# Time mixing: chunks dealt out one or two to a step, value rows spread as rounded halves, and the bonus added by GpSimd before one centring product

## The chip, the cores and the metric

The kernel runs on one core of a Trainium2 chip. The number compared is device microseconds of one execution. Before the change three executions gave 3112.59, 3116.45 and 3120.53 us, so the median is 3116.45 us. One further execution was profiled: it took 3117.54 us, with a span of 3115.7 us inside it.

## The reference, cut to what matters

The reference is an RWKV-like layer followed by a cross-attention block. Only its first part, time mixing, is touched. Batch is 16, length 128, width 512 in 32 heads of 16.

```python
w = jnp.exp(-jnp.exp(time_decay + jnp.tanh(x5[:, :, 1] @ decay_w1) @ decay_w2))
r = (x5[:, :, 3] @ Wr.T).reshape(b, l, H, S)
k = (x5[:, :, 0] @ Wk.T).reshape(b, l, H, S)
v = (x5[:, :, 2] @ Wv.T).reshape(b, l, H, S)
g = jax.nn.silu(x5[:, :, 4] @ Wg.T)
def step(s, rkvw):
    r_t, k_t, v_t, w_t = rkvw
    a = k_t[:, :, :, None] * v_t[:, :, None, :]
    out = jnp.einsum('bhk,bhkd->bhd', r_t, u * a + s)
    return (a + w_t[:, :, :, None] * s, out)
a4 = att.reshape(b, l, H, S)
m = jnp.mean(a4, axis=-1, keepdims=True)
var = jnp.mean((a4 - m) ** 2, axis=-1, keepdims=True)
att = ((a4 - m) * jax.lax.rsqrt(var + EPS)).reshape(b, l, E) * gn_w + gn_b
x = x + att * g @ Wo.T
```

The part `u * a` of the output is called the bonus in the kernel: r·k·u is summed over a head and multiplied by v.

## The kernel before, in words

`time_mix` works on four batches at a time (a quad, `q` = 0 to 3). A quad has a front (normalisation, the low-rank mixes, the value product `stage`), a **body** of 32 steps `t`, and a joint that finishes quad `q` while it starts quad `q + 1`; after quad 3 there is a closing instead. Channels lie on partitions; the 512 channels make four groups (`g` or `f`, 0 to 3), and steps `8g` to `8g + 7` belong to group `g`. One step handles two of the 16 value rows `d` of a head, for all 512 columns (4 batches x 128 positions).

Each engine has its own program, written out in this order by hand, and they meet by semaphores only. In a step `t` of the body:

- TensorE: `spread(t + 2)` copies two value rows to all partitions of a head: two fp32 products with 32 rows (`tm_spread_v`) into two of the four banks of `tm_vb`. It waits until the scan of step `t` has read these banks (`scanned`). Then come, by a table of conditions on `t`, other pieces: `accumulate(t - 2)` in even steps (sum over the rows of a head, `tm_pick_k`), `bonus(f)` at `8f + 1`, halves (two chunks each) of the projections `receptance`, `key` and `gate` into the one bank `tm_pj1`, `centred(f)` at `8f + 10`, `variance(f)` at `8f + 12`, `unpacks(f)` at `8f + 14`. A chunk is one fp32 product of 128 x 128 by 512 columns, four to a projection. `centred` subtracts the head's mean by a product with `tm_centre`, once for the scan's part (`tm_h5`) and once for the bonus (`tm_bb`), added in PSUM.
- ScalarE: writes the initial state into the banks (`tm_vb<-tm_s`, line 421), which lets VectorE start step `t`. Between these, in order, it takes projections and other results out of PSUM: `bonus(f)` at `8f + 2`, `attended(f)` at `8f + 10`, `square(f)` at `8f + 12`, `deviation(f)` at `8f + 14`, `gate`, `receptance`, `key`.
- VectorE: the product with k (line 567) and two scans (line 572) for each step. After some steps `inverse(f)` (a reciprocal, `8f + 14`) and `gated(f)` (`8f + 15`).
- GpSimd: multiplies the state by r (line 302), and at some steps makes r·k (`receptance_key`) or the bonus product (`bonus`).

The tile `tm_vb` has two pairs of banks, so the values for step `t + 2` can only be spread once step `t` has been scanned. The first and last quads are written out, quads 1 and 2 run in a loop.

Of the kernel before, what the change touches and what calls it, by code (L numbers as in the profile page):

```python
# [25 lines left out]
P = 128  # L26
# [59 lines left out]
def time_mix(nc, io, x2):  # L86
# [3 lines left out]
    with ExitStack() as ctx:  # L90
# [22 lines left out]
        spread_v = sb("spread_v", [P, 4, P])  # L113
        prev = sb("prev", [P, EC, B])
# [56 lines left out]
        vb_full, s0_set, scanned = sem("vb_full"), sem("s0_set"), sem("scanned")  # L171
        rs_ready, rs_used, att_ready = sem("rs_ready"), sem("rs_used"), sem("att_ready")
# [71 lines left out]
        def _(gp):  # L244
# [23 lines left out]

            def bonus(q, f):
                gp.wait_ge(bonus_out, q * 4 + (f + 1))  # L270
                if f < 2 and q > 0:
                    gp.wait_ge(cent_full, q * 4)
                gp.tensor_tensor(quad3(bb[:, f % 2, :]), quad3(ew[:]), vv[:, f, :, 1:L + 1], ALU.mult).then_inc(bonus_used, 1)

            gp.wait_ge(w_ready, 2)
            gp.memset(wd[:], 0.0).then_inc(ready, 1)
            for q in range(NQ):
# [19 lines left out]
                for t in range(STEPS):  # L297
# [5 lines left out]
                    for f in range(EC):  # L303
                        if t == 8 * f - 2:
                            receptance_key(q, f)
                        if t == 8 * f + 2:
                            bonus(q, f)

        @block.scalar
        def _(act):  # L310
# [60 lines left out]
            def body(q, first):  # L371
# [31 lines left out]

                def bonus(f):
# [9 lines left out]
                for f in range(EC):  # L414
                    evacuate(f)
                key(0)
                act.wait_ge(s0_in, q * 16 + 16)
                for t in range(STEPS):
# [5 lines left out]
                    for f in range(EC):  # L424
                        if t == 8 * f + 2:
                            bonus(f)
                        if f > 0 and t == 8 * f - 4:
                            receptance(f)
                        if f > 0 and t == 8 * f - 2:
                            key(f)  # L430
                        if t == (8, 16, 24, 28)[f]:
# [39 lines left out]
        def _(v):  # L471
# [82 lines left out]
            def body(q, first):  # L554
# [5 lines left out]
                for t in range(STEPS):  # L560
# [69 lines left out]
        def _(pe):  # L630
# [68 lines left out]
            def body(q, first):  # L699
# [34 lines left out]
                def spread(t):  # L734
# [1384 lines left out]
```

## Time and profile before

| | us |
|---|---|
| median of 3 executions | 3116.45 (3112.59 to 3120.53) |
| the profiled execution, its own time | 3117.54 |
| its span | 3115.7 |
| body of quad 0, from the first step's product to the last scan | 72.6 to 199.3 |
| body of quad 1 | 258.1 to 387.2 |
| body of quad 2 | 449.2 to 578.3 |
| body of quad 3 | 637.0 to 766.8 |
| end of time mixing, start of the next phase | about 794 |

Over the whole span TensorE is busy 94%, VectorE 58%, ScalarE 37% and GpSimd 15%. These shares are governed by what comes after time mixing and say little of the bodies. In the body of quad 1 (129.1 us) TensorE is busy 113.0 us, VectorE 117.1, GpSimd 82.0 and ScalarE 27.7, at a mean granted TensorE clock of 0.88 of full speed.

### The profile page before, as it was taken

To read this page: it belongs to the slowest core of one execution; us is meant where nothing else is said; L and a number is where in the kernel's file an instruction comes from. 1 tells how busy PE (TensorE), PEld (TensorE's weight loads), DVE (VectorE), ACT (ScalarE), POOL (GpSimd) and SP (SyncE) were. 2 spreads that over 40 slices of the span, in tenths; PEclk is the share of its full clock that TensorE was granted. 3 is DMA by queue.
4 is the path that set the end of the run, shared out by engine and by line. 5 is a ranking of instruction groups with operands and counts; after the bars stand their busy time and mean duration, and the time that the engine had idled before them with its cause. 6 is when DMAs were issued, how large, how long until landed. Compare 5 with 4: busy or idle time off the path is not lost.

```text
span 3115.7 us, 41240 instructions
## 1 busy us (share of the span) xinstructions
PE 2939.4 (94%) x14960; PEld 2212.5 (71%) x14960; DVE 1809.3 (58%) x2660; ACT 1145.5 (37%) x2509; POOL 480.6 (15%) x331
## 2 busy tenths in 40 slices
PE   6889899898696999999999999999999999999899
PEld 3233243332475888888888887878888888888787
DVE  6989979887674544446444456464444554444644
ACT  3222222221343434345343444343434444343432
POOL 1745636455000000001000000010000000000100
PEclk8989899898898999999999999999999999999999
DMA  4000010100224111111111111121111111101011
GB/s 143 7 20 33 11 42 10 32 13 1 97 91 151 65 54 37 54 37 34 52 37 54 37 51 54 47 72 55 37 54 37 54 38 44 47 30 44 27 51 57
DMA packets 54784, 148.76 MB, mean 48 GB/s; under 512 B 6256, under 2 KB 7536, under 8 KB 53584
## 3 DMA queue, kind: packets, MB, share of 16 engines
q1 hardware_dynamic: 51824, 143.80, 13.9%
q0 software_dynamic: 2880, 3.94, 0.6%
q8 instruction: 45, 0.74, 0.1%
q14 instruction: 35, 0.29, 0.0%
HBM read 131.20 MB, written 12.58 MB: 46 GB/s over the span
## 4 chain that ended last, share of the span: by engine, by line
PE 66%; DVE 2%; ACT 1%; issue 0%; DMA 0%; ACTq 0%; DVEq 0%
PE ca_ps L60 19%; PE ca_ps L62 19%; PE ca_ps L61 19%; PE ca_ps L1892 4%; PE ca_ps L1876 4%; PE ca_ps L1884 2%; PE ca_ps L1918 1%; DVE ca_stats L68 0%; DVE ca_xres L1653 0%; DVE ca_ctx_lo L1684 0%; DMA ca_xres<-in_ctxT 0%; DVE ca_wq_lo L1611 0%; ACT ca_sk L1569 0%; DVE ca_h_lo L1678 0%; ACT L1569 0%
## 5 line engine op out<-in xcount | busy, mean ns | idle before, releaser
L1653 DVE TENSOR_TENSOR ca_xres<-ca_xres,ca_ps 128x512 f32<-128x512 f32 x384 | 263.8, 687 | 244.4 <-PE ca_ps L62 239.4
L1440 ACT ACTIVATE ca_pr<-ca_ps,ca_nb 128x129 f32<-128x129 f32 x512 | 181.7, 368 | 510.9 <-DVE ca_nb L1636 510.7
L60 PE MATMUL ca_ps<-ca_h_hi,ca_wq_hi 128*128 128x512 f32 x768 | 313.0, 408 | 4.7 <-DVE ca_h_lo L1678 4.2
L572 DVE TENSOR_TENSOR_SCAN tm_xn<-tm_wd,tm_vb 128x512 f32<-128x512 f32 x256 | 298.5, 1207 | 8.9 <-POOL tm_xf L302 0.4
L62 PE MATMUL ca_ps<-ca_h_hi,ca_wq_lo 128*128 128x512 f32 x768 | 303.0, 394 | 0.0
L61 PE MATMUL ca_ps<-ca_h_lo,ca_wq_hi 128*128 128x512 f32 x768 | 300.9, 392 | 0.0
L60 PE MATMUL ca_ps<-ca_wv_hi,ca_ctx_hi 128*128 128x256 f32 x1024 | 297.8, 291 | 0.0
L62 PE MATMUL ca_ps<-ca_wv_hi,ca_ctx_lo 128*128 128x256 f32 x1024 | 287.4, 281 | 0.0
L61 PE MATMUL ca_ps<-ca_wv_lo,ca_ctx_hi 128*128 128x256 f32 x1024 | 287.2, 280 | 0.0
L60 PE MATMUL ca_ps<-ca_wo_hi,ca_ct_hi 128*128 128x512 f32 x640 | 253.5, 396 | 0.2 <-DVE ca_xres L1653 0.2
L61 PE MATMUL ca_ps<-ca_wo_lo,ca_ct_hi 128*128 128x512 f32 x640 | 252.7, 395 | 0.0
L62 PE MATMUL ca_ps<-ca_wo_hi,ca_ct_lo 128*128 128x512 f32 x640 | 252.5, 394 | 0.0
L1393 POOL TENSOR_TENSOR ca_dv<-ca_bvr 128x256 f32<-128x256 f32 x32 | 23.7, 740 | 1453.7 <-DVE ca_v L1621 1443.7
L60 PE MATMUL ca_ps<-ca_ctx_hi,ca_wk_hi 128*128 128x512 f32 x512 | 203.7, 398 | 22.4 <-DVE ca_wk_lo L1616 18.4
L62 PE MATMUL ca_ps<-ca_ctx_hi,ca_wk_lo 128*128 128x512 f32 x512 | 202.7, 396 | 0.0
L61 PE MATMUL ca_ps<-ca_ctx_lo,ca_wk_hi 128*128 128x512 f32 x512 | 201.4, 393 | 0.0
L746 PE MATMUL tm_vb<-tm_vv,tm_spread_v 32*128 32x512 f32 x512 | 149.9, 689 | 52.2 <-DVE tm_xn L572 52.1
L61 PEld LDWEIGHTS ca_ps<-ca_wv_lo,ca_ctx_hi 128*128 128x128 f32 x1024 | 194.6, 190 | 0.0
L62 PEld LDWEIGHTS ca_ps<-ca_wv_hi,ca_ctx_lo 128*128 128x128 f32 x1024 | 194.1, 190 | 0.0
L60 PEld LDWEIGHTS ca_ps<-ca_wv_hi,ca_ctx_hi 128*128 128x128 f32 x1024 | 192.7, 188 | 0.0
L567 DVE TENSOR_TENSOR tm_vb<-tm_vb,tm_kk 128x1024 f32<-128x1024 f32 x128 | 155.5, 1215 | 33.1 <-ACT tm_vb L421 32.8
L60 PEld LDWEIGHTS ca_ps<-ca_h_hi,ca_wq_hi 128*128 128x128 f32 x768 | 145.1, 189 | 33.6 <-issue 5.4
(233 smaller groups left out, 5832.9 us busy)
## 6 DMA issues: line engine op xcount, KB each, us to landing
ca_sq<-in_wq SPq DMA_DIRECT2D x49, 512.0 KB, 5.4
ca_so<-in_wo SPq DMA_DIRECT2D x48, 512.0 KB, 3.5
ca_sk<-in_wk SPq DMA_DIRECT2D x33, 512.0 KB, 6.6
ca_sv<-in_wv SPq DMA_DIRECT2D x32, 512.0 KB, 3.6
ca_bvr<-in_bvb SPq DMA_DIRECT2D x32, 256.0 KB, 3.9
tm_xq<-in_x SPq DMA_DIRECT2D x16, 256.0 KB, 2.7
tm_xres<-in_x SPq DMA_DIRECT2D x4, 1024.0 KB, 5.7
x_dram<-tm_xres SPq DMA_DIRECT2D x4, 1024.0 KB, 4.6
```

The source lines that it names most:

```text
L60: pe.matmul(out, lhs[0], rhs[0], start=first, stop=False)
L61: pe.matmul(out, lhs[0], rhs[1], start=False, stop=False)
L62: return pe.matmul(out, lhs[1], rhs[0], start=False, stop=last)
L567: v.tensor_tensor(pair4, pair4, kk[:, g:g + 1, :, 0:L].broadcast_to([P, 2, 4, L]), ALU.mult).then_inc(scanned, 1)
L572: v.tensor_tensor_scan(state[t % 2][:, d, :], wd[:, g].rearrange("p b t -> p (b t)"), pair[:, d, :], 0.0, ALU.mult, ALU.add).then_inc(scan ...
L746: ins = pe.matmul(vb[:, 2 * (t % 2) + e, :], spread_v[k:k + 32, u, :], vv[k:k + 32, g, :, 0:L], start=True, stop=True)
L1440: ins = act.activation(pr[hd][:, b, :], ps[:, BANK_SC + b // 2, o:o + KW], ACT.Exp, bias=nbs[hd][:, b:b + 1], scale=SCALE, accum_out=sms[h ...
L1653: v.tensor_tensor(xres[U.h][:, U.quad * 4 + b, :], xres[U.h][:, U.quad * 4 + b, :], ps[:, BANK_O + b % 2, :], ALU.add).then_inc(o_out, 1)
L1876: ins = pe.matmul(ps[:, BANK_SC + b // 2, o:o + KW], qT[hd][:, b * L:(b + 1) * L], kT[hd][:, b, :], start=True, stop=True)
L1884: ins = pe.transpose(ps[:, BANK_TR, b * L:(b + 1) * L], pr[hd][:, b, 0:L], ident[:])
L1892: ins = pe.matmul(ps[:, BANK_PV, b * L:(b + 1) * L], vT[A.quad][:, b, hd * P:(hd + 1) * P], pT[hd][:, b * L:(b + 1) * L], start=True, stop ...
L1918: ins = pe.transpose(ps[:, LN_BANKS[c], b * P:(b + 1) * P], lt[:, b, c * P:(c + 1) * P], ident[:])
```

## The change

Four things move in `time_mix`, all inside the bodies and their ends.

- `spread` for groups 1 to 3 no longer takes fp32 values. ScalarE rounds the value rows to `x_hi` (`value_hi`, at `8f - 6`), GpSimd makes the rest `x_lo` (`value_lo`, at `8f - 5`), and TensorE does four fp32r products of 32 rows instead of two fp32 ones, halves added in PSUM. A rounded copy `spread_r` of the spreading matrix is made once.
- Projections are given out in chunks: at most two in a step, and `receptance`, `key` and `gate` stand one step earlier, or end one step later, than they did.
- GpSimd adds the bonus to the scan's part (`add_bonus`, at `8f + 10`, for group 3 after the last step), and `centred` becomes one product, at `8f + 11`.
- `square`, `variance`, `deviation`, `inverse`, `unpacks` and `gated` stand one step later.

```diff
+            def value_lo(q, c):
+                gp.wait_ge(v_hi_ready, q * 3 + c)
+                gp.tensor_tensor(quad3(x_lo[:, c, :]), vv[:, c, :, 0:L], quad3(x_hi[:, c, :]), ALU.subtract).then_inc(v_split_ready, 1)
+            def add_bonus(q, f):
+                gp.wait_ge(att_ready, q * 4 + (f + 1))
+                gp.wait_ge(bonus_used, q * 8 + (f * 2 + 2 if f < 3 else 6))
+                gp.tensor_tensor(h5[:], h5[:], bb[:, f % 2, :], ALU.add).then_inc(bonus_used, 1)
...
-                    for f in range(EC):
+                    for f in reversed(range(EC)):
                         if t == 8 * f - 2:
                             receptance_key(q, f)
                         if t == 8 * f + 2:
                             bonus(q, f)
+                        if t == 8 * f + 10:
+                            add_bonus(q, f)
+                        if f > 0 and t == 8 * f - 5:
+                            value_lo(q, f)
+                add_bonus(q, 3)
...
+                def value_hi(c):
+                    act.activation(quad3(x_hi[:, c, :]), vv[:, c, :, 0:L], ACT.Copy).then_inc(v_hi_ready, 1)
...
-                        if f > 0 and t == 8 * f - 4:
+                        if f > 0 and t == 8 * f - 5:
                             receptance(f)
+                        if f > 0 and t == 8 * f - 6:
+                            value_hi(f)
...
-                        if t == (8, 16, 24, 28)[f]:
+                        if t == (9, 17, 25, 27)[f]:
                             gate(f)
...
             def centred(q, f):
-                pe.wait_ge(att_ready, q * 4 + (f + 1))
-                pe.wait_ge(bonus_used, q * 4 + (f + 1))
-                pe.matmul(mx[f % 2][:], centre[:], h5[:], start=True, stop=False)
-                pe.matmul(mx[f % 2][:], centre[:], bb[:, f % 2, :], start=False, stop=True).then_inc(cent_full, 1)
+                pe.wait_ge(bonus_used, q * 8 + (2 * f + 3 if f < 3 else 8))
+                pe.matmul(mx[f % 2][:], centre[:], h5[:], start=True, stop=True).then_inc(cent_full, 1)
...
+                        for part in (x_hi, x_lo):
+                            for e in range(2):
+                                k = 32 * (2 * (t % 2) + e)
+                                ins = pe.matmul(vb[:, 2 * (t % 2) + e, :], spread_r[k:k + 32, u, :], part[k:k + 32, g, :],
+                                                start=part is x_hi, stop=part is x_lo)
...
-                        if f > 0 and t in (8 * f - 7, 8 * f - 6):
-                            receptance(f, t - (8 * f - 7))
-                        if f > 0 and t in (8 * f - 5, 8 * f - 4):
-                            key(f, t - (8 * f - 5))
-                        if f < 3 and t in (8 * f + 5, 8 * f + 6):
-                            gate(f, t - (8 * f + 5))
-                        if f == 3 and t in (25, 26):
-                            gate(f, t - 25)
-                        if t == 8 * f + 10:
+                        if f > 0 and t in (8 * f - 8, 8 * f - 7):
+                            receptance(f, ((0, 1), (2, 3))[t - (8 * f - 8)])
+                        if f > 0 and t in (8 * f - 6, 8 * f - 5, 8 * f - 4):
+                            key(f, ((0, 1), (2,), (3,))[t - (8 * f - 6)])
+                        if f < 3 and t in (8 * f + 5, 8 * f + 6, 8 * f + 7):
+                            gate(f, ((0, 1), (2,), (3,))[t - (8 * f + 5)])
+                        if f == 3 and t in (24, 25):
+                            gate(f, ((0, 1), (2, 3))[t - 24])
+                        if t == 8 * f + 11:
                             centred(q, f)
```

TensorE in steps 7 and 8 of a body, before: `spread` (746) for steps 9 and 10, and `accumulate` (666).

```order
L746 MATMUL tm_vb<-tm_vv,tm_spread_v 128x512 [waits tm_scanned]
L746 MATMUL tm_vb<-tm_vv,tm_spread_v 128x512
L746 MATMUL tm_vb<-tm_vv,tm_spread_v 128x512 [waits tm_scanned]
L746 MATMUL tm_vb<-tm_vv,tm_spread_v 128x512
L666 MATMUL tm_mx<-tm_sx,tm_pick_k 32x512 [waits tm_rs_ready]
L666 MATMUL tm_mx<-tm_sx,tm_pick_k 32x512 x3
```

The same two steps now (776 is `spread` by halves, 690 `accumulate`, 782 a chunk of a projection).

```order
L776 MATMUL tm_vb<-tm_x_hi,tm_spread_r 128x512 [waits tm_scanned]
L776 MATMUL tm_vb<-tm_x_hi,tm_spread_r 128x512
L776 MATMUL tm_vb<-tm_x_lo,tm_spread_r 128x512 x2
L782 MATMUL tm_pj<-tm_xg,tm_wg 128x512
L776 MATMUL tm_vb<-tm_x_hi,tm_spread_r 128x512 [waits tm_scanned]
L776 MATMUL tm_vb<-tm_x_hi,tm_spread_r 128x512
L776 MATMUL tm_vb<-tm_x_lo,tm_spread_r 128x512 x2
L690 MATMUL tm_mx<-tm_sx,tm_pick_k 32x512 [waits tm_rs_ready]
L690 MATMUL tm_mx<-tm_sx,tm_pick_k 32x512 x3
L782 MATMUL tm_pj<-tm_xr,tm_wr 128x512 [waits tm_g_ready]
L782 MATMUL tm_pj<-tm_xr,tm_wr 128x512
```

One chunk of gate 0 came into step 7 and two chunks of receptance 2 into step 8, where there were none.

ScalarE around step 10, before: gate 0 (410), the state of steps 9 and 10 (421), `attended(0)` (335), `bonus(1)` (406), the state of steps 11 and 12.

```order
L410 ACTIVATE tm_gg<-tm_pj 128x512 [waits tm_g_full]
L421 ACTIVATE tm_vb<-tm_s 128x8 [waits tm_vb_full] x2
L335 ACTIVATE tm_h<-tm_mx 128x512 [waits tm_bonus_full,tm_rs_used]
L406 ACTIVATE tm_ew<-tm_pj 128x512 [waits tm_bonus_full]
L421 ACTIVATE tm_vb<-tm_s 128x8 [waits tm_vb_full] x2
```

Now (443 is the state, 351 `attended`, 425 `bonus`, 421 `value_hi`, 411 `receptance`).

```order
L429 ACTIVATE tm_gg<-tm_pj 128x512 [waits tm_g_full]
L443 ACTIVATE tm_vb<-tm_s 128x8 [waits tm_vb_full]
L351 ACTIVATE tm_h<-tm_mx 128x512 [waits tm_bonus_full,tm_rs_used]
L425 ACTIVATE tm_ew<-tm_pj 128x512 [waits tm_bonus_full]
L421 ACTIVATE tm_x_hi<-tm_vv 128x512
L443 ACTIVATE tm_vb<-tm_s 128x8 [waits tm_vb_full]
L411 ACTIVATE tm_rr<-tm_pj 128x512 [waits tm_r_full]
```

A third copy, `value_hi(2)`, stands between the bonus and the state of step 11; gate 0 moved from step 8 to step 9.

VectorE at the end of a body, before: the last scan pairs (572), the product of step 31 (567), `inverse(2)` (536), and the joint's first statistics.

```order
L572 SCALAR_TENSOR_TENSOR tm_xn<-tm_wd,tm_vb 128x512
L536 RECIPROCAL tm_grs<-tm_grs 128x128 [waits tm_gstd_ready]
L567 TENSOR_TENSOR tm_vb<-tm_vb,tm_kk 128x1024 [waits tm_s0_set]
L572 SCALAR_TENSOR_TENSOR tm_xn<-tm_wd,tm_vb 128x512 [waits tm_scanned,tm_rs_ready]
L572 SCALAR_TENSOR_TENSOR tm_xn<-tm_wd,tm_vb 128x512
L482 BN_STATS tm_stats<-tm_xq 128x6 [waits tm_x_in0]
```

And now, with lines 591, 596, 560 and 506 in their places.

```order
L596 SCALAR_TENSOR_TENSOR tm_xn<-tm_wd,tm_vb 128x512
L591 TENSOR_TENSOR tm_vb<-tm_vb,tm_kk 128x1024 [waits tm_s0_set]
L596 SCALAR_TENSOR_TENSOR tm_xn<-tm_wd,tm_vb 128x512 [waits tm_scanned,tm_rs_ready]
L596 SCALAR_TENSOR_TENSOR tm_xn<-tm_wd,tm_vb 128x512
L560 RECIPROCAL tm_grs<-tm_grs 128x128 [waits tm_gstd_ready]
L506 BN_STATS tm_stats<-tm_xq 128x6 [waits tm_x_in0]
```

The reciprocal of group 2 moved behind the last scan. TensorE's `unpacks(2)`, which waits for it, stands as before just ahead of the four `output` products that follow the last scan.

## Rows read from the trace of the kernel before

**Rows 1.** The page: span, and the scan's group (mean ns, idle before).
```profile
span 3115.7 us, 41240 instructions
...
L572 DVE TENSOR_TENSOR_SCAN tm_xn<-tm_wd,tm_vb 128x512 f32<-128x512 f32 x256 | 298.5, 1207 | 8.9 <-POOL tm_xf L302 0.4
```

**Rows 2.** VectorE's waits, 72.6 to 766.8 us: total us, times, longest.
```profile
DVE tm_vb L567 <- ACT tm_vb L421: 32.8, 28, 2.2
...
DVE tm_pj L541 <- PE tm_pj L690: 4.1, 8, 0.7
...
DVE tm_xn L572 <- POOL tm_xf L302: 0.4, 2, 0.2
```

**Rows 3.** The same view of quad 1's body alone.
```profile
DVE tm_vb L567 <- ACT tm_vb L421: 9.2, 8, 1.9
```

**Rows 4.** Timeline of VectorE, products of steps 25, 26, 27, quad 1: start, us.
```profile
358.71 1.21 DVE L567 TENSOR_TENSOR tm_vb<-tm_vb,tm_kk 128x1024 f32<-128x1024 f32 x1
...
362.20 1.21 DVE L567 TENSOR_TENSOR tm_vb<-tm_vb,tm_kk 128x1024 f32<-128x1024 f32 x1
...
367.71 1.23 DVE L567 TENSOR_TENSOR tm_vb<-tm_vb,tm_kk 128x1024 f32<-128x1024 f32 x1 [1.93 <-ACT tm_vb L421]
```

**Rows 5.** Timeline of TensorE and ScalarE there; an fp32 product shows as x2.
```profile
362.34 2.08 PE L746 MATMUL tm_vb<-tm_vv,tm_spread_v 32*128 32x512 f32 x4 [1.19 <-DVE tm_xn L572]
...
364.35 2.08 PE L732 MATMUL tm_pj<-tm_h,tm_head_sum_u 128*128 128x512 f32 x2
...
366.52 0.60 ACT L335 ACTIVATE tm_h<-tm_mx 128x512 f32<-128x512 f32 x1 [6.31 <-PE tm_pj L732]
367.01 0.59 ACT L406 ACTIVATE tm_ew<-tm_pj 128x512 f32<-128x512 f32 x1
...
367.49 0.19 ACT L421 ACTIVATE tm_vb<-tm_s 128x8 f32<-128x8 f32 x1
```

**Rows 6.** Timeline of TensorE, steps 9 and 10 of quad 0, at full clock.
```profile
108.67 1.13 PE L746 MATMUL tm_vb<-tm_vv,tm_spread_v 32*128 32x512 f32 x4 [1.44 <-DVE tm_xn L572]
109.73 1.13 PE L732 MATMUL tm_pj<-tm_h,tm_head_sum_u 128*128 128x512 f32 x2
110.69 1.88 PE L751 MATMUL tm_pj<-tm_xr,tm_wr 128*128 128x512 f32 x4
112.50 1.13 PE L746 MATMUL tm_vb<-tm_vv,tm_spread_v 32*128 32x512 f32 x4
113.56 1.07 PE L666 MATMUL tm_mx<-tm_xf,tm_pick_k 128*32 128x512 f32 x8
```

**Rows 7.** Timeline of TensorE, two fp32r products of the value stage, full clock.
```profile
251.62 0.39 PE L61 MATMUL tm_vb<-tm_x_lo,tm_w_hi 128*128 128x512 f32 x1
251.85 0.39 PE L62 MATMUL tm_vb<-tm_x_hi,tm_w_lo 128*128 128x512 f32 x1
```

**Rows 8.** Windows: PE, PEld, DVE, ACT, POOL busy, then granted clock.
```profile
261.70:265.10 3.40, 1.29 (x5) 0.30 (x4) 3.37 (x4) 0.78 (x2) 2.20 (x2) 1.00 0.00 0
...
292.40:295.80 3.40, 2.03 (x14) 0.46 (x12) 3.37 (x4) 0.18 (x1) 2.26 (x2) 1.00 0.00 0
295.80:299.20 3.40, 3.40 (x7) 1.18 (x4) 2.89 (x3) 0.22 (x1) 2.25 (x2) 0.50 0.00 0
```

**Rows 9.** Groups by line, 60 to 770 us, GpSimd and ScalarE: busy, mean ns.
```profile
L302 POOL TENSOR_TENSOR tm_xf<-tm_xn,tm_rr 128x1024 f32<-128x1024 f32 x64 | 150.4, 2352 | 96.2 <-DVE tm_xn L572 73.3 <-PE tm_mx L666 22.9
...
L273 POOL TENSOR_TENSOR tm_bb<-tm_ew,tm_vv 128x512 f32<-128x512 f32 x16 | 18.9, 1181 | 0.0
...
L329 ACT ACTIVATE tm_x_hi<-tm_xf 128x512 fp32r<-128x512 f32 x12 | 7.6, 631 | 37.1 <-DVE tm_xf L520 37.1
```

**Rows 10.** Timeline of the end of quad 1's body and the joint's start.
```profile
382.74 0.93 DVE L536 RECIPROCAL tm_grs<-tm_grs 128x128 f32<-128x128 f32 x1
...
383.75 2.08 PE L690 MATMUL tm_pj<-tm_grs,tm_unpack 128*128 128x128 f32 x8
...
387.21 5.76 PE L695 MATMUL tm_vb<-tm_wo,tm_vv 128*128 128x512 f32 x8 [1.39 <-DVE tm_xn L572]
```

More of the change, by code:

```diff
@@ L113, in time_mix @@
         spread_v = sb("spread_v", [P, 4, P])
+        spread_r = sb("spread_r", [P, 4, P], FR)
         prev = sb("prev", [P, EC, B])
@@ L415, in body @@
                     evacuate(f)
+                if first:
+                    act.wait_ge(const_in, N_CONST)
+                    act.activation(spread_r[:], spread_v[:], ACT.Copy).then_inc(w_hi_ready, 1)
                 key(0)
@@ L740, in spread, with project, key @@
                     elif t % 8 == 0:
-                        pe.wait_ge(f_free, q * 4 + (g + 1))
+                        pe.wait_ge(v_split_ready, q * 3 + g)
+                        if first and g == 1:
+                            pe.wait_ge(w_hi_ready, 4)
                     if t >= 2:
                         pe.wait_ge(scanned, q * (3 * STEPS) + 3 * (t - 1))
-                    for e in range(2):
-                        k = 32 * (2 * (t % 2) + e)
-                        ins = pe.matmul(vb[:, 2 * (t % 2) + e, :], spread_v[k:k + 32, u, :], vv[k:k + 32, g, :, 0:L], start=True, stop=True)
+                    if g == 0:
+                        for e in range(2):
+                            k = 32 * (2 * (t % 2) + e)
+                            ins = pe.matmul(vb[:, 2 * (t % 2) + e, :], spread_v[k:k + 32, u, :], vv[k:k + 32, 0, :, 0:L], start=True, stop=True)
+                    else:
+                        for part in (x_hi, x_lo):
+                            for e in range(2):
+                                k = 32 * (2 * (t % 2) + e)
+                                ins = pe.matmul(vb[:, 2 * (t % 2) + e, :], spread_r[k:k + 32, u, :], part[k:k + 32, g, :],
+                                                start=part is x_hi, stop=part is x_lo)
                     ins.then_inc(vb_full, 1)
-                def project(w, x, f, half, full):
-                    for c in (2 * half, 2 * half + 1):
+                def project(w, x, f, chunks, full):
+                    for c in chunks:
                         ins = pe.matmul(pj[1][:], w[:, c, f * P:(f + 1) * P], x[:, c, :], start=c == 0, stop=c == EC - 1)
-                    if half == 1:
+                    if EC - 1 in chunks:
                         ins.then_inc(full, 1)
-                def key(f, half):
-                    if half == 0:
+                def key(f, chunks):
+                    if 0 in chunks:
                         if f > 0:
@@ L763, in key, with receptance @@
                                 pe.wait_ge(wkr_in, 32)
-                    project(wk, xk, f, half, k_full)
-                def receptance(f, half):
-                    if half == 0:
+                    project(wk, xk, f, chunks, k_full)
+                def receptance(f, chunks):
+                    if 0 in chunks:
                         if f > 1:
@@ L774, in receptance, with gate @@
                             pe.wait_ge(xf_ready, q * 24 + 24)
-                    project(wr, xr, f, half, r_full)
-                def gate(f, half):
-                    if half == 0:
+                    project(wr, xr, f, chunks, r_full)
+                def gate(f, chunks):
+                    if 0 in chunks:
                         if f < 3:
@@ L784, in gate @@
                             pe.wait_ge(late_in, 32)
-                    project(wg, xg, f, half, g_full)
+                    project(wg, xg, f, chunks, g_full)
                 stage(0)
@@ L802, in body @@
                 spread(1)
-                receptance(0, 0)
-                receptance(0, 1)
+                receptance(0, (0, 1, 2, 3))
                 for t in range(STEPS):
```

19 lines of the change are left out of this document (10 added, 9 removed).

## The prediction

> **What bounds the kernel now.** I read the page first. Its busy shares (TensorE 94%) belong to the attention phase, which the change doesn't touch, so I went to time mixing, the first 794 us, and there to the four bodies. In a body VectorE has the longest chain of its own: one product and two scans of 1.21 us a step [rows 1], and when nothing holds it the products of two steps start 3.49 us apart (362.20 - 358.71) [rows 4]. 32 such steps, two reciprocals and two `gated` between them are what a body must take. What it takes beyond that stands in VectorE's waits. Over all four bodies it waits 32.8 us for ScalarE's write of the initial state, 4.1 us for `unpacks`, and 0.4 us for GpSimd [rows 2]; quad 1 alone has 9.2 us of the first kind [rows 3]. These 37.3 us are the most that a change of the other engines' order can give back inside the bodies.
>
> Then I followed one of the waits back. Step 27 of quad 1 started 5.51 us after step 26 instead of 3.49 [rows 4]. Its links, all from [rows 4, 5]: 0.14 us from the end of scan 25 to the start of `spread(27)`, 2.01 until the bonus product can start, 2.08 for that product, 0.09 to ScalarE, 0.49 for `attended`, 0.48 for the bonus copy, 0.22 for the state and the step to VectorE. Together 5.51 us, the measured distance, so nothing else takes part. The state of step 27 isn't late because it needs the bonus; it stands behind it in ScalarE's order, and the bonus product stands behind `spread` in TensorE's. At full clock [rows 6] the first two TensorE links are 1.06 (109.73 - 108.67) and 1.13 us, and the same chain is 0.14 + 1.06 + 1.13 + 0.09 + 0.49 + 0.48 + 0.22 = 3.61 us: a stall of 0.12. So the long stalls are stalls of the granted clock. It fell to half (1.2 GHz) after stretches with little for TensorE to do: after one with 1.29 of 3.40 us busy at the start of quad 1's body, and after 2.03 of 3.40 around steps 8 and 9; the stretch behind the latter ran at 0.50 of full speed [rows 8]. These holes are in the table of steps: before, the steps 7, 8, 15, 16 and 23, 24 have no chunk, and step 0 none either.
>
> **The spread by halves.** Before: two fp32 products in different row strips, 1.06 us to the next instruction at full clock [rows 6]. An fp32 chunk takes 0.90 us (two in 112.50 - 110.69), an fp32r product of the same 512 columns 0.23 (251.85 - 251.62) [rows 6, 7]. The pair costs 1.06 for one product's 0.90, so what is not streaming is about 0.2. Two fp32r products one behind the other in each strip, the strips side by side, are 0.46 + 0.2 = 0.66 us, my value. No row shows an fp32r product in 32 rows. Bounds: 0.46 if the fixed part vanishes, 1.56 if all four run strictly one after the other at their full 0.39 [rows 7]. I take 0.66 because the fp32 pair in these very strips does run side by side.
>
> The Trainium skill (TensorE: Matmul & The Clock Gate, Part 3) says that a weight load goes beside running products only when it is for another row strip. The high and low half share a strip, so by that rule each low product would first wait out its load, and a spread would be nearer 0.9 us. The trace speaks against a full wait: an fp32 product also has two records in the same strip, and the pair still costs only 0.16 more than one chunk. With 0.9 the two chains at steps 11 and 19 are 0.24 longer in each body, about 2 us in all, and the result would be 3096.
>
> **The chunks.** With `accumulate` at 1.00 and `bonus` at 0.96 to the next start [rows 6], TensorE's load now is: step 0: 1.06 + 1.81 = 2.9; steps 8 to 10: 0.66 + about 1.0 + 1.81 = 3.5, just the floor of 3.49; steps 11 to 14: 2.6 to 3.0; steps 15, 16: 2.6 and 3.5; step 7 only 0.66 + 0.90 = 1.6. So the hole at a body's start is filled, and the ones at steps 15 and 23 nearly so, but step 7 keeps one: about 2.0 us busy in 3.4 around it, or less, as in the stretch before the fall at 295.8 [rows 8]. I expect the clock to fall once in each body there, and to come back after one saturated stretch, as the 3.40 us from 295.80 were; at half speed that costs 1.7 us of TensorE's work. Steps 8 and 9 have no slack to make this good, so it arrives whole in step 11.
>
> **ScalarE's third copy.** `value_hi` takes 0.63 us, about 0.50 in a row of copies [rows 5, 9]. It stands ahead of the states of steps 3, 11 and 19. Full-clock chains now: step 11 and 19: 0.14 + 0.66 + 1.13 + 0.09 + 0.49 + 0.48 + 0.50 + 0.22 = 3.71, stall 0.22 each. Step 3 (fp32 spread, no `attended`): 0.14 + 1.06 + 1.13 + 0.09 + 0.50 + 0.50 + 0.22 = 3.64, stall 0.15. Step 27 (no `value_hi`): 3.21, none. With the fallen clock step 11 adds 1.75: 1.97.
>
> **GpSimd.** It gets eight more passes a quad: four adds at about 1.18 and three `value_lo`, at most 1.3 [rows 9]. They are hidden by its idle time: 8 x 2.35 + 4 x 1.2 = 23.6 us in eight steps of at least 27.9. The tight place is steps 10 and 11: counted from scan 10, the products for steps 10, 11 and 12 end at 2.5, 7.2 and 10.9 us (0.15 + 2.35, then bonus, add, 2.35, then `value_lo`, 2.35), and scans 12, 13 and 14 want them at 4.6, 8.1 and 11.6. Nothing waits, with 0.7 us to spare. Behind the add waits `centred`, until 5.0 us; TensorE idles there and the next spread is not due until 7.1. If the cover went, each place would cost about 1 us, 12 in all.
>
> **The later pieces.** `inverse` and `gated` one step later keep their work, but `unpacks` now has a whole step to finish before `gated` wants it, so the 4.1 us go. At a body's end it is the reverse: `inverse(2)` stood before the last scans and now stands behind them, and TensorE must do `unpacks(2)` after it and before the four outputs. The scans end 0.93 earlier, and 2.08 of `unpacks` at half clock come in front of the 5.76 us of outputs and accumulation [rows 10] that the joint waits for: 1.15 us more each for three joints. The closing has the same, less one chunk-sized centring product of 0.90: 0.25. In the joints that product hides behind VectorE's shift chain and gives nothing. Bounds: nothing, if the clock comes back earlier thanks to the added work, and 2.1 us a joint if it comes back one stretch later. The one copy for `spread_r`, 0.6 us, lies in a wait of ScalarE for TensorE.
>
> **The sum.** Given back: 37.3. New stalls for each body: 0.15 + 1.97 + 0.22 = 2.34, and 0.25 for small ones of the kind that the chains don't resolve; four bodies: 10.4. Ends: 3 x 1.15 + 0.25 = 3.7. Net 37.3 - 10.4 - 3.7 = 23.2 us. The profiled execution took 3117.5, which gives 3094.3; the median lies 1.1 us under it, so I forecast 3094, 0.7% less.
>
> **Rivals.**
> 1. The clock holds past step 7. For: in quad 0 the clock stood full at steps 7 to 10, as the full-clock durations of [rows 6] show, although these steps had holes before too. Against: step 7 is emptier than any step next to it. Then 4 x 1.75 fewer: 3087, and some 3 us less if the joints also start at full clock: 3084.
> 2. The clock falls more often. The work that halves take away (0.4 us in 24 steps of a quad) is also what kept TensorE busy; at steps 15 and 23 `unpacks` now waits 0.9 us for the reciprocal in a step that VectorE's own extra work makes 4.4 us long. If the clock falls there too, the chains of steps 19 and 27 get about 1.7 each: 4 x 3.4 = 14 more, 3108.
> 3. The change doesn't reach its purpose because GpSimd's late products bind at steps 12 to 14: 12 places at about 1 us give 3106. Against: the 0.7 us to spare.
> 4. Slower. The four 32-row fp32r products run one after the other. At 1.56 us a spread, eight steps cost TensorE 8 x 1.56 + 4 x 1.0 + 12 x 0.90 + 0.96 + 0.90 and 1.5 for `variance` and `unpacks` = 30.7, with no hole left for waits, and steps 8 to 10 are 4.4 us each. VectorE's own need is 8 x 3.49 + 2.4 = 30.3. The three groups of a body would lose 2.7 us in steps 8 to 10 and again in 16 to 18 and 24, 25, and about as much in the chains at half clock: some 12 us a body against 9.3 now, and with the ends 3129. It decides at a spread of about 1.4 us; below that the filled holes win.
>
> **Chances.** The forecast's way 0.52 (3088 to 3101 alone), rival 1 0.18, rivals 2 and 3 together 0.21, rival 4 0.09. The range goes from rival 1's 3083 to 3109, just past rival 2. A measurement of this kernel tells about 0.3% (9 us) from no change, so faster ends at 3107: the forecast, rival 1 and half of 2 and 3 make 0.80; same 0.13, slower 0.07.
>
> **What would show it.** A spread with about 0.66 us to the next instruction. VectorE's wait for the state down from 32.8 to about 10 us, most of it at step 11, and after a fall of the granted clock around step 8; none at steps 13, 21, 27 and 29. No wait of `gated` for `unpacks` in the bodies. About 1.2 us more from the last scan to ScalarE's `attended(3)`. I am wrong if spreads take over 1 us, if half-clock stretches come at steps 16 and 24, or if VectorE waits for GpSimd by more than 2 us.

## The result and the profile after

| | before | after |
|---|---|---|
| median, us | 3115.75 (4 executions) | 3088.84 (3087.40 to 3094.17, 4 executions) |
| ratio to before | | 0.9916, 95% interval 0.9901 to 0.9932 |
| the profiled execution | 3117.54 | 3094.17, span 3091.6 |
| bodies of quads 0 to 3, us | 126.7, 129.1, 129.1, 129.8 | 122.3, 119.2, 117.0, 121.1 |
| from each body to the next (the last: to the next phase) | 58.8, 62.0, 58.7, 27.5 | 60.6, 64.8, 60.6, 28.6 |
| start of the first body | 72.6 | 75.5 |
| start of the next phase | 794.3 | 769.8 |

By medians the kernel is 0.84% faster, 26.9 us; 3094 with a range of 3083 to 3109 was forecast. The four bodies became 35.1 us shorter, what lies between and behind them 7.6 us longer, and the first body began 2.9 us later. That last difference isn't the change's: the same kernel profiled once more (below) began it at 73.1.

VectorE's waits in time mixing after the change, the view of [rows 2]: total us, times, longest.

```profile
DVE tm_vb L591 <- ACT tm_vb L443: 8.4, 8, 3.3
DVE tm_xn L522 <- PE tm_mx L690: 6.4, 3, 2.6
...
DVE tm_pj L565 <- PE tm_pj L712: 2.2, 1, 2.2
...
DVE tm_xn L596 <- POOL tm_xf L313: 0.4, 2, 0.2
```

The wait for the initial state fell from 32.8 to 8.4 us, and the one for `unpacks` inside the bodies is gone (the single 2.2 stands in the closing). New is 6.4 us in the three joints (line 522), where `output` and `accumulate` come late; before it was 2.6. GpSimd is waited for no more than before.

A stretch in which the granted clock is 0.50 (1.2 GHz) is called a fall from here on, and a step of TensorE with little in it a hole. The fall at the start of a body is gone, as was worked out: before, the clock fell 7 to 8 us into each of the four bodies (at 80.8, 265.1, 456.2 and 644.0 us); now it stays full there in all four, in quad 1 from 258.4 to 292.0 us.

Most of the 8.4 us, 7.2, is left at step 11; the rest is at step 19. TensorE in steps 7 and 8 of quad 0 and at the start of step 9 (start, length, what, idle before):

```profile
104.02 0.50 PE L776 MATMUL tm_vb<-tm_x_hi,tm_spread_r 32*128 32x512 f32 x2 [0.68 <-DVE tm_xn L596]
104.36 0.40 PE L776 MATMUL tm_vb<-tm_x_lo,tm_spread_r 32*128 32x512 f32 x2
104.68 1.12 PE L782 MATMUL tm_pj<-tm_xg,tm_wg 128*128 128x512 f32 x2
107.58 0.70 PE L776 MATMUL tm_vb<-tm_x_hi,tm_spread_r 32*128 32x512 f32 x2 [1.77 <-DVE tm_xn L596]
108.07 0.63 PE L776 MATMUL tm_vb<-tm_x_lo,tm_spread_r 32*128 32x512 f32 x2
108.64 1.94 PE L690 MATMUL tm_mx<-tm_sx,tm_pick_k 128*32 128x512 f32 x8
110.50 3.78 PE L782 MATMUL tm_pj<-tm_xr,tm_wr 128*128 128x512 f32 x4
114.21 0.64 PE L776 MATMUL tm_vb<-tm_x_hi,tm_spread_r 32*128 32x512 f32 x2
```

The first three rows are step 7. The spread takes 104.68 - 104.02 = 0.66 us to the next instruction, then one chunk, then 1.77 us of nothing. From 107.58 to the end of these chunks the products take twice their time: `accumulate` 1.86 us to the next start instead of 1.00, two chunks 3.71 instead of 1.81. ScalarE's copies and VectorE's product of step 11 follow late:

```profile
116.24 0.60 ACT L351 ACTIVATE tm_h<-tm_mx 128x512 f32<-128x512 f32 x1 [7.31 <-PE tm_pj L754]
116.73 0.59 ACT L425 ACTIVATE tm_ew<-tm_pj 128x512 f32<-128x512 f32 x1
117.21 0.63 ACT L421 ACTIVATE tm_x_hi<-tm_vv 128x512 fp32r<-128x512 f32 x1
117.73 0.18 ACT L443 ACTIVATE tm_vb<-tm_s 128x8 f32<-128x8 f32 x1
```
```profile
111.00 1.21 DVE L591 TENSOR_TENSOR tm_vb<-tm_vb,tm_kk 128x1024 f32<-128x1024 f32 x1
...
117.94 1.23 DVE L591 TENSOR_TENSOR tm_vb<-tm_vb,tm_kk 128x1024 f32<-128x1024 f32 x1 [3.30 <-ACT tm_vb L443]
```

It is the chain of [rows 5] again, with `value_hi` as a third copy in it. The windows over these steps (as [rows 8]):

```profile
100.90:104.30 3.40, 2.72 (x16) 0.74 (x14) 3.30 (x4) 0.18 (x1) 3.34 (x3) 1.00 0.02 5
104.30:107.70 3.40, 1.63 (x8) 0.43 (x8) 3.30 (x4) 2.06 (x3) 2.20 (x2) 1.00 0.00 0
107.70:111.10 3.40, 3.40 (x13) 0.99 (x14) 3.30 (x4) 0.18 (x1) 2.33 (x1) 0.50 0.00 0
111.10:114.50 3.40, 3.40 (x6) 0.96 (x6) 3.30 (x3) 0.00 (x0) 2.35 (x1) 0.50 0.00 0
114.50:117.90 3.40, 3.40 (x12) 1.32 (x12) 0.14 (x1) 1.66 (x5) 2.85 (x2) 1.00 0.00 0
```

TensorE is busy 1.63 of 3.40 us around step 7, and the two stretches behind run at 0.50 (1.2 GHz). VectorE waits at step 11 of quads 0 to 3 for 3.30, 1.88, 0.23 and 1.77 us; in quad 2, the one of 0.23, the clock stayed full through these steps, and around the same step 7 TensorE was busy 2.25 and 2.14 of 3.40:

```profile
469.50:472.90 3.40, 2.25 (x8) 0.59 (x6) 3.37 (x4) 1.44 (x2) 3.40 (x3) 1.00 0.00 0
472.90:476.30 3.40, 2.14 (x13) 0.75 (x14) 3.37 (x4) 0.81 (x3) 2.26 (x2) 1.00 0.00 0
```

The end of quad 1's body, TensorE and then VectorE (before: [rows 10]):

```profile
378.49 2.08 PE L712 MATMUL tm_pj<-tm_grs,tm_unpack 128*128 128x128 f32 x8 [3.39 <-DVE tm_grs L560]
380.36 5.50 PE L717 MATMUL tm_vb<-tm_wo,tm_vv 128*128 128x512 f32 x8
385.79 1.07 PE L690 MATMUL tm_mx<-tm_sx,tm_pick_k 128*32 128x512 f32 x8
```
```profile
377.50 0.93 DVE L560 RECIPROCAL tm_grs<-tm_grs 128x128 f32<-128x128 f32 x1
...
387.13 0.18 DVE L522 COPY tm_xn<-tm_prev 128x16 f32 x1 [2.55 <-PE tm_mx L690]
```

The reciprocal is now behind the last scan, TensorE stands idle for it, and `unpacks` and the outputs run at half clock until the joint's VectorE has waited 2.55 us.

### The profile page after: what moved, and what is told of

Read it like the earlier page. It is cut to its first block, busy times and chain, and to the rows that moved or that the text cites. A ratio compares the mean times of both kernels' runs of the same rounds, so it can differ in the third digit from the quotient of the medians.

```text
span 3091.6 us, 41223 instructions
## 1 busy us (share of the span) xinstructions
PE 2888.0 (93%) x14928; PEld 2196.8 (71%) x14928; DVE 1805.6 (58%) x2660; ACT 1150.9 (37%) x2522; POOL 514.6 (17%) x359
## 4 chain that ended last, share of the span: by engine, by line
PE 66%; DVE 2%; ACT 1%; issue 0%; DMA 0%; ACTq 0%; DVEq 0%
PE ca_ps L60 19%; PE ca_ps L62 19%; PE ca_ps L61 19%; PE ca_ps L1922 4%; PE ca_ps L1906 4%; PE ca_ps L1914 2%; PE ca_ps L1948 1%; DVE ca_stats L68 0%; DVE ca_xres L1683 0%; DVE ca_ctx_lo L1714 0%; DMA ca_xres<-in_ctxT 0%; DVE ca_wq_lo L1641 0%; ACT ca_sk L1599 0%; DVE ca_h_lo L1708 0%; ACT L1599 0%
## 5 line engine op out<-in xcount | busy, mean ns | idle before, releaser
L62 PEld LDWEIGHTS ca_ps<-ca_h_hi,ca_wq_lo 128*128 128x128 f32 x768 | 144.8, 189 | 33.3
L61 PEld LDWEIGHTS ca_ps<-ca_h_lo,ca_wq_hi 128*128 128x128 f32 x768 | 145.3, 189 | 28.1
```

What stands on the lines that cost most here:

```text
L61: pe.matmul(out, lhs[0], rhs[1], start=False, stop=False)
L62: return pe.matmul(out, lhs[1], rhs[0], start=False, stop=last)
```

## Experiments: the parts of the change

Each version is an edit of the changed kernel, or of the one before where said. The kernel before was timed beside each of three sets: its median was 3115.24 beside the changed kernel again, step 7 with two chunks, the early inverse and all three together; 3115.85 beside the four versions that take the change apart; 3114.68 beside the other four. The four versions that take the change apart ran on another chip than the other eight, beside the kernel before there. "State wait" is VectorE's wait for the initial state, the first row of the view above; the "period" of a step is the time from the product of the step before to its own. Medians whose intervals overlap are called apart only where the trace shows where they part.

**The changed kernel again**, no edit.

> The changed kernel once more, beside the variants. Its median was 3088.8 us, four runs from 3087.4 to 3094.2, and in its profile the falls of the granted clock decide the wait at step 11 (3.30, 1.88, 0.23 and 1.77 us in quads 0 to 3). If the falls are a matter of where the chip's clock stands against the program, this run gives 3086 to 3094 with other numbers at the steps 11, sum 5 to 10 us; if they are fixed by the program, the same four numbers come back within 0.1 us.

3087.95 us, 0.9916 (0.9902 to 0.9929), span 3081.7. State wait 6.2 us; the periods of step 11 are 5.31, 5.46, 3.81 and 5.44, and the first clock fall behind step 7 was 3.4 us long and not 6.8. The numbers of step 11 did not all come back, so the program alone does not fix where the falls lie and how long they last. Two profiles of one kernel differ by 2.2 us in the state wait and 2.4 in the opening, and one version below, with the same steps 0 to 29, had 12.7 us: a state wait from one profile says little, medians more.

**Only the halves**: the kernel before, with `value_hi`, `value_lo`, `spread_r` and the four fp32r products.

```diff
-    for e in range(2): matmul(vb, spread_v, vv[.., g, ..])
+    for part in (x_hi, x_lo):
+        for e in range(2): matmul(vb, spread_r, part[.., g, :])
```

> Only the spreads by halves, in the old table. TensorE has 0.4 us less to do in 24 steps of a quad, and the holes at steps 7, 8, 15, 16, 23 and 24 become emptier. If holes and the clock rule: the falls stay or come oftener, waits of 1.5 to 2 us at steps 11, 19, 27 remain, the 4.1 us for the unpacking remain, time 0 to 8 us under the kernel before. Rival (TensorE's load rules): 12 us or more under it.

3097.63 us, 0.9946 (0.9928 to 0.9964). State wait 22.5 us in 21 places, none longer than 1.6; the falls stay where they were, at the chains of steps 11, 19 and 27:

```profile
DVE tm_vb L583 <- ACT tm_vb L435: 22.5, 21, 1.6
```

In the old table halves alone give 18 us, where 0 to 8 were expected and the rival said 12 or more. The falls behaved as expected; what they cost did not. At half clock a spread by halves took 1.06 us to the next start (107.58 to 108.64 above), where the whole one took 2.01 [rows 5], so each chain behind a fall is shorter. The wait of `gated` for `unpacks`, expected to remain, is gone too, with `unpacks` at its old step.

**Whole fp32 spreads**: the changed kernel without the halves.

```diff
-    act value_hi at 8f - 6, POOL value_lo at 8f - 5, four fp32r products
+    two fp32 products for all groups
```

> The changed kernel with fp32 spreads for all groups, no value_hi and value_lo. A spread then costs 1.06 us instead of 0.66 to the next instruction. If the halves pay for themselves (steps 8 to 10 hold 1.06 + 1.0 + 1.8 = 3.9 us of work against 3.49, so the lag grows by 0.4 a step): waits of 1 to 2 us at steps 11, 19 and 27, time 6 to 12 us over the changed kernel. Rival (more streaming keeps the clock up, and the third copy is gone): no falls behind step 7, the waits of step 11 shrink, time within 3 us of the changed kernel or under it.

3084.85 us, 0.9904 (0.9882 to 0.9925). State wait 7.3 us in 5 places, the longest 3.7. The halves gave nothing on top of the new table, where 6 to 12 us had been expected of them. The rival's time held, and its reason in part: behind step 7 the clock still fell in quads 0 (6.8 us) and 3 (3.4 us).

**Two centring products**: `add_bonus` taken out, `centred` as before but at its new step.

```diff
-    matmul(mx, centre, h5 + bb)
+    matmul(mx, centre, h5, start=True, stop=False)
+    matmul(mx, centre, bb, start=False, stop=True)
```

> The changed kernel with the bonus added in PSUM by a second centring product again, no add on GpSimd. The second product costs TensorE 0.9 us in steps 11, 19 and 27, which hold 2.6 to 3.0 us of work, so it fits. Expectation: no wait in the bodies grows by more than 0.2 us, the time is within 2 us of the changed kernel, 1 us more at the closing. Rival (the single product is what made room): waits at steps 12 and 20, 5 us or more slower.

3089.6 us, 0.992 (0.9899 to 0.9941). State wait 9.1. No difference in time that can be told, as expected.

**Only the table**: both edits together, so that of the change the dealing of chunks and the later places are left.

> Only the new places of chunks and later pieces: fp32 spreads, two centring products. If the filled steps and the room before gated are most of the gain: 12 to 20 us under the kernel before. Rival (the halves are most of it): under 8 us.

3087.36 us, 0.9912 (0.9891 to 0.9933). State wait 8.4 us, in 4 places, the longest 3.8. The numbers in the table alone give all of the gain: 28.5 us, where the whole change gives 26.9 and 12 to 20 had been expected. Halves and table take from the same waits: of the 32.8 us of state wait the halves alone leave 22.5, the table alone 8.4 and both 8.4 (6.2 when profiled again), and either alone takes the 4.1 us of `gated`. So 18 and 28 don't add up to 46. What the dealing of chunks gives and what the later places give was not measured apart.

## Experiments: what is still waited for

**Step 7 with two chunks**: gate 0 dealt as one, one and two chunks in steps 5, 6 and 7.

```diff
-    gate(f, ((0, 1), (2,), (3,))[t - (8 * f + 5)])
+    gate(f, (((0,), (1,), (2, 3)) if f == 0 else ((0, 1), (2,), (3,)))[t - (8 * f + 5)])
```

> Only gate 0 is dealt out otherwise: one chunk in step 5, one in step 6, two in step 7 instead of two, one, one. Theory (the hole of step 7 lets the clock fall and the lag lands in step 11): no half-clock stretch between steps 7 and 12 of any quad, the wait of step 11 goes to 0.2 to 0.5 us in each quad, VectorE's wait for the state falls from about 8.4 to 2 or 3 us, the time is 4 to 6 us under the changed kernel's. Rival (the wait of step 11 is ScalarE's third copy and the saturated steps 8 to 10, whatever the clock does): the waits stay at 1.8 us or more where they were, the time is the same within 2 us. Step 5 now has one chunk, as step 3 has; if that is a hole of its own, a fall comes at step 6 or 7 instead and nothing is won.

3085.17 us, 0.9903 (0.9888 to 0.9918), state wait 4.8. That is 2.8 us under the changed kernel, with intervals that overlap; 4 to 6 had been expected. The falls didn't go; in three quads they moved two steps earlier, behind the hole that the edit had opened. Quad 0:

```profile
96.20:99.60 3.40, 1.93 (x8) 0.51 (x6) 3.30 (x4) 0.18 (x1) 2.19 (x2) 1.00 0.22 77
99.60:103.00 3.40, 3.40 (x13) 0.86 (x12) 3.30 (x4) 0.18 (x1) 3.34 (x3) 0.50 0.02 5
103.00:106.40 3.40, 3.33 (x10) 0.97 (x8) 3.30 (x4) 1.49 (x3) 2.33 (x1) 0.99 0.00 0
```

There the fall lasted 3.4 us and step 11 waited for nothing. In quads 1 and 3 the moved fall lasted 6.8 us (280.5 to 287.3 and 642.3 to 649.1), and step 11 still waited 1.75 and 1.58 us. Moving the hole two steps earlier helps against a short fall and not against a long one.

**Redundant work in step 7**: the products that spread the rows of step 9 are done three times. Nothing is taken away.

```diff
-    for part in (x_hi, x_lo):
+    for part in ((x_hi, x_lo) if t != 9 else (x_hi, x_lo, x_hi, x_lo, x_hi, x_lo)):
```

> The changed kernel with work added and none taken away: in step 7 TensorE does the four products that spread the rows of step 9 three times instead of once (the result is the same, 2 x 0.46 = 0.92 us of redundant products at full clock). Theory (step 7, with 1.6 us of work in a step of 3.49, is what lets the granted clock fall just ahead of step 8, 9 or 10, and this is what step 11 pays for): the falls behind step 7 go or come elsewhere, the period of step 11 is 3.7 in every quad, VectorE's waits for the state over four bodies are 2 us or less instead of 6 to 8, and the time is 4 to 6 us under the changed kernel: 3082 to 3085. Rival (the clock falls for another reason than this step, or step 7 has no slack): falls behind step 7 as before, waits as before or longer, 3088 to 3092.

3080.92 us, 0.9894 (0.9877 to 0.9911). The same windows as after, over steps 7 to 9 of quad 0, and the state wait:

```profile
101.90:105.30 3.40, 2.56 (x16) 1.18 (x14) 3.30 (x4) 1.88 (x3) 2.26 (x1) 1.00 0.00 0
105.30:108.70 3.40, 3.40 (x16) 1.07 (x16) 3.30 (x4) 0.36 (x2) 2.37 (x1) 1.00 0.00 0
108.70:112.10 3.40, 3.40 (x11) 1.35 (x10) 3.30 (x4) 1.39 (x3) 2.37 (x1) 1.00 0.00 0
```
```profile
DVE tm_vb L591 <- ACT tm_vb L443: 1.3, 4, 0.5
```

The falls behind step 7 are gone in all four quads, the periods of step 11 are 3.75, 3.81, 3.81 and 3.74, and the kernel is 7 to 8 us under the changed one, with 32 more products; its slowest execution, 3082.24, is faster than the fastest of the changed kernel's nine, 3084.30. Waits and time came out as the theory said, the time 1 us under its range. This is the strongest evidence that the emptiness of step 7 is what step 11 pays for. The bodies took 119.1, 117.0, 117.4 and 119.2. The falls in the last steps of a body, 17.1 to 20.5 us long, are still there, and so are three of 3.4 us behind steps 15 and 23; they cost the bodies at most the 0.5 us at a step 19.

**`value_hi` and `value_lo` at 8f - 4**, behind the state of step 11.

```diff
-    if f > 0 and t == 8 * f - 6: value_hi(f)      # value_lo at 8f - 5
+    if f > 0 and t == 8 * f - 4: value_hi(f)      # value_lo at 8f - 4
```

> The changed kernel with one edit: the rounding of the value rows on ScalarE and the rest on GpSimd stand at step 8f-4, so that the third copy no longer stands between the bonus copy and the state of step 11. Theory (a stall at step 11 is the chain through the bonus product, stretched by a fallen clock): the third copy is 0.50 us of that chain, so the period of step 11 falls by up to 0.5 us in each quad where the clock has fallen, and by 0.2 where it hasn't; together 1 to 2 us in four bodies, which three thousandths of the time hide: 3086 to 3089, interval over the changed kernel's. Rival (what counted in the combined version was this edit): the state waits go nearly to nothing, as there, and the time is 3082 or less.

3082.22 us, 0.9896 (0.9879 to 0.9912). The waits of step 19 are gone and the state wait is 6.4 us in 3 places, step 11 of quads 0, 2 and 3. Like set beside like, the third copy is worth what was expected: behind a fall of 6.8 us the period of step 11 in quad 0 is 6.38 instead of 6.94, and behind one of 3.4 us in quad 3 it is 4.88 instead of 5.41. The median lies 5.7 us under the changed kernel's, more than expected, and the intervals overlap; the trace shows at most 2 us of it. What the rest is stays open. The rival's time came out, its reason, state waits near nothing, did not.

**The inverse of group 2 early**: `deviation`, `inverse` and `unpacks` of group 2 in step 30 and not in 31, so that they precede the last scans, as they did before the change.

```diff
-    if t == 8 * f + 15: inverse(q, f)
+    if t == (15, 23, 30)[f]: inverse(q, f)
```

> Only the pieces of group 2 at the end of a body go back: deviation, inverse and unpacks in step 30 instead of 31. Theory (the unpacking ahead of the four outputs lengthens the joint): the wait of VectorE's copy for the last accumulation goes from 6.4 us over three joints back to about 2.6, the scan of step 31 ends 0.9 later, and the time is 1.0 to 1.2 us less for each of four ends, 4 to 5 us in all. Rival (the joint's length is set by when the clock comes back and VectorE's chain behind it): within 2 us of the changed kernel.

3082.9 us, 0.9895 (0.988 to 0.991). The joints' wait fell from 6.4 us to one of 0.3, below the 2.6 of the kernel before:

```profile
DVE tm_vb L591 <- ACT tm_vb L443: 12.7, 7, 3.4
...
DVE tm_xn L522 <- PE tm_mx L690: 0.3, 1, 0.3
```

The stretches behind the bodies are 58.4, 59.6, 58.2 and 26.5 us, 11.9 less than after; 3.7 of that is the reciprocal that went back into the bodies. In this profile the falls behind step 7 came in all four quads and lasted 6.8 us in three of them, and the state wait came to 12.7, though the edit touches nothing near step 7; the median still gained 5, as expected.

## Experiments: a faster version

**All three**: step 7 with two chunks, `value_hi` later, the inverse early.

> Both edits, and value_hi and value_lo in step 8f - 4 instead of 8f - 6 and 8f - 5, so that no third copy stands before the states of steps 3, 11 and 19. If the three parts add up: 4 to 6 us, 4 to 5 us, and 0.3 to 0.5 us at up to eleven places, 2 to 3 us, so 10 to 13 us under the changed kernel, about 3077. If the falls of the clock only move elsewhere, 4 to 6 us less. Slower than the changed kernel only if the later low halves come too late for the first spread of a group: then TensorE's first spread at steps 6, 14 and 22 waits for GpSimd, up to 0.5 us each.

3071.55 us (3070.59 to 3071.92), 0.9861 (0.9846 to 0.9876): 44 us under the kernel before, 16 under the changed one, where 10 to 13 had been expected. VectorE never waits for the state. The clock still falls in each quad but one behind the emptier step 5:

```profile
95.60:99.00 3.40, 1.93 (x10) 0.53 (x12) 3.30 (x4) 0.04 (x1) 2.19 (x2) 0.86 0.32 82
99.00:102.40 3.40, 3.40 (x12) 0.83 (x10) 3.38 (x3) 0.14 (x1) 3.33 (x3) 0.64 0.00 0
102.40:105.80 3.40, 3.29 (x16) 1.14 (x18) 3.31 (x3) 2.21 (x4) 2.21 (x2) 1.00 0.00 0
```

There three steps lie between it and the bonus chain, and steps 6 and 7 have room to make it good. A fall costs only what is due before TensorE has caught up. The three falls of this profile lasted 3.4 us each; one of 6.8, which reached step 11 with two chunks alone, did not come here, so it isn't shown that this version would bear it. The four executions lie within 1.4 us of each other.

**The same with fp32 spreads**:

> The version of the dealing of chunks and the early inverse that was fastest so far, but with whole fp32 spreads instead of rounded halves (no third copy on ScalarE, no rest on GpSimd, 0.40 us more of TensorE in 24 steps of a quad). Theory A (the halves are what gives TensorE the room that the even dealing needs, so that steps 8 to 10 fit in 3.49 us): without them steps 8 to 10 need 1.06 + 1.0 + 1.81 = 3.87 us each, states wait again, 6 to 10 us in all, and the time is 3077 to 3081. Theory B (the halves gave nothing on top of the dealing, as in the changed kernel): within 3 us of the combined version, 3069 to 3075.

3081.45 us, 0.9889 (0.9873 to 0.9906), 10 above. The hole of quad 0 is the same, 1.94 of 3.40, but now the clock stays at half for three stretches, and VectorE waits in steps 9, 10 and 11:

```profile
96.70:100.10 3.40, 1.94 (x8) 0.52 (x6) 3.30 (x4) 0.18 (x1) 2.20 (x2) 1.00 0.26 77
100.10:103.50 3.40, 3.40 (x12) 0.37 (x10) 3.30 (x4) 0.18 (x1) 3.33 (x3) 0.50 0.02 5
103.50:106.90 3.40, 3.40 (x10) 1.01 (x6) 3.28 (x3) 0.00 (x0) 2.33 (x1) 0.50 0.00 0
106.90:110.30 3.40, 3.40 (x5) 1.18 (x4) 2.22 (x2) 1.46 (x2) 2.35 (x1) 0.50 0.00 0
```
```profile
107.97 1.23 DVE L587 TENSOR_TENSOR tm_vb<-tm_vb,tm_kk 128x1024 f32<-128x1024 f32 x1 [1.09 <-ACT tm_vb L441]
...
112.28 1.23 DVE L587 TENSOR_TENSOR tm_vb<-tm_vb,tm_kk 128x1024 f32<-128x1024 f32 x1 [0.63 <-ACT tm_vb L441]
...
118.33 1.23 DVE L587 TENSOR_TENSOR tm_vb<-tm_vb,tm_kk 128x1024 f32<-128x1024 f32 x1 [2.38 <-ACT tm_vb L441]
```

Halves that give nothing on top of the changed kernel's table give 10 us once step 11's wait has been taken away; that much is measured, and theory B is out. Theory A, that whole spreads leave steps 8 to 10 no room, holds in part. Without a fall, in quads 1 to 3, step 11 waits 0.51, 0.52 and 0.38 us, where with halves it waits for nothing. The other 4.1 of the 5.5 us of state wait stand behind the one long fall of quad 0, which came again in the next version. Why the clock stays low for 3.4 us in one case and 10.2 in the other, and whether whole spreads have a part in it, the runs don't show.

**And with two centring products as well**:

> As the one before, and the centring is again two products, with no bonus add on GpSimd: of the change only the dealing of chunks and the later places are left, with the early inverse and step 7's chunk. If the single centring product gives nothing (as with whole fp32 spreads it cost nothing to undo it), it stands within 3 us of the one before; if it carries work that TensorE has no room for, 0.90 us of it in four places of a quad, it stands 4 to 10 us above.

3083.36 us, 0.9896 (0.9879 to 0.9912), 2 above the one before. The single centring product isn't worth anything that can be measured here either.

## Why the prediction was right

- **What bounds.** That VectorE's waits in the bodies were what could be given back held: 28.5 of the 37.3 us were (32.8 to 8.4, and 4.1 to nothing; GpSimd's 0.4 stayed). But 37.3 was not the most to be had. A wait costs its step a little more than the view lists: step 27 of quad 1 came 5.51 - 3.49 = 2.02 us late with 1.93 listed [rows 4]. With all three edits and the reciprocals back in their places the four bodies took 473.5 us instead of 514.7, which is 41.2 less. After the change the bodies' 35.1 us are the 28.5, 3.7 of reciprocals moved out, and 2.9 that the sum had no term for. Of these, 28 waits fewer (38 before, 10 after) at 0.09 us each are about 2.5, an estimate from step 27.
- **The spread** is 0.66 us, as worked out. The Trainium skill (TensorE: Matmul & The Clock Gate, Part 3), where it lists what overlaps, has a weight load go beside running products only when it is for another row strip; by the estimate in the prediction that would have made the spread about 0.9. The measured 0.66 decides against it for these products of 32 rows, and the loads of the low halves show it directly. They start at 104.13, while the products of the high halves in the same strips, from 104.02 on, still run:

```profile
104.13 0.19 PEld L776 LDWEIGHTS tm_vb<-tm_x_lo,tm_spread_r 32*128 32x128 f32 x2
```

- **The hole in step 7 and the wait in step 11.** Forecast: one fall a body there, and 1.97 us. Measured: 3.30, 1.88, 0.23, 1.77, together 7.2 for 7.9. The fall came in three quads of four and lasted two stretches in one; the sizes of single places were off both ways, so the nearness of the total is partly luck. That a fall lasts one stretch was read from the one at 295.8 us alone: the trace of before also had one of 6.8 us (360.7 to 367.5, the one behind the very wait that was taken apart) and one of 10.2 (381.2 to 391.4). The run with redundant work shows the cause and not only the size.
- **Step 19 and step 3.** 0.22 forecast, 0.28, 0.50, 0.15 and 0.29 measured at step 19; nothing that counts at step 3, where 0.15 was forecast. New stalls in all: 8.4 for 10.4.
- **GpSimd** holds nothing up, as forecast: 0.4 us as before, so rival 3 is out. The closing's `add_bonus` lies beside TensorE's outputs.
- **The ends.** 3.7 us forecast. The stretches behind the bodies grew by 7.6, of which 4 x 0.93 = 3.7 is the reciprocal, leaving 3.9. The working had a flaw that didn't show in its sum: it set the reciprocal's 0.93 against `unpacks`, but `unpacks` waits for the reciprocal just as it would for the scans. Measured, the outputs start 2.77 us after the last scan at all four ends, where it was 0.05; less the 0.93 by which the scans end earlier this is 1.8 us, not 1.15. Part of it came back because less of the outputs ran at half clock: in quad 0 the clock was full again 2.7 us into them, before only after 4.2. Joint by joint the 1.15 came out as 0.9, 1.9 and 1.0, and the closing's 0.25 as 0.2: a near hit by luck. From the last scan to `attended(3)` it is 1.8 to 2.5 us more, where 1.2 was given as the sign. The early inverse shows that this order is what the joints' 6.4 us come from.
- **The sum.** 23.2 forecast, 23.4 in the profiled execution, which holds the 2.9 us of a late first body and so agrees by luck; by medians 26.9. In the bodies, reciprocals left aside, 26.9 were forecast and 31.4 measured. Of these 4.5 the stalls, 8.4 instead of 10.4, are 2.0, and what waits cost beyond their listed time is the 2.9; GpSimd's 0.4, which stayed, goes the other way. Three slips bear on nothing: 3116.45 less 23.2 is 3093.2 and not 3094, GpSimd got seven more passes a quad and not eight, and rival 4's own numbers give 3131 and not 3129.
- **The rivals.** The first (the clock holds past step 7) came true in one quad of four, and redundant work made it true in all: 3081, where 3084 to 3087 was worked out. The second has its falls (3.4 us each, at 141.8 and 172.6, 322.7 and 353.5, and at 684.6 us, behind steps 15 and 23, the first and second reciprocal steps, of quads 0 and 1, and behind step 15 of quad 3). Half-clock stretches at steps 16 and 24 were named as a sign of being wrong, and this sign did come. But steps 19 and 27 had room enough: step 19 waited 0.50 us at most and step 27 not at all, so the price of 1.7 us each is what failed in that rival, and the sign was set too strictly. The fourth falls with the 0.66.
- **Not foreseen**: that the halves and the single centring product add nothing to this table. The prediction costed them as parts of one design; what the halves are worth depends on which wait ends last.

## What to carry to other kernels

When a granted clock falls after a nearly empty step, look at what is due in the two or three steps behind it: move work into the hole, or move the hole to where the following steps have slack and nothing on the critical chain is due. Two edits that fill the same lack don't add up; measure each alone and with the other, and once the last wait is gone measure again, since a part that gave nothing can then give ten microseconds. Where falls of the clock decide, price an edit by medians and not by one profile: the same steps gave state waits from 6.2 to 12.7 us. A reduction that is put off by one step is free inside a loop and is paid at its end, where nothing is left to hide it.

## What the runs showed of the hardware

More work made the kernel faster: 32 redundant products gave back 7 to 8 us, by keeping the granted clock at full (2.56 busy of 3.40 us in the stretch of step 7 where 1.63 had been). The same hole doesn't always give the same fall. Behind step 7 of the changed kernel the clock stayed at 0.50 of full speed for 6.8 us in one profile and 3.4 in the other (quad 0), and behind the emptier step 5 for 3.4, 6.8 or 10.2 us by version and quad, with TensorE busy without a gap meanwhile. Which length comes isn't explained by anything tried here. And four fp32r products of 32 rows, two in each row strip, take 0.66 us, where two fp32 ones in the same strips take 1.06; their weight loads ran beside products of the same strips.
